# Channel sums in three halving additions and one place wait for two products, in a recommendation tower kernel

## The reference, cut to what matters

```python
# x0, xk: [batch, fields, 16]; w0: [39, 39, 128]; w1, w2: [39, 64, 128]
z = jnp.einsum('bhd,bkd,hks->bsd', x0, xk, W) + b[None, :, None]
z = jax.nn.relu(z)                      # [batch, 128, 16]
if idx != n_layers - 1:
    half = z.shape[1] // 2
    xk = z[:, :half, :]                 # input of the next layer
    direct.append(z[:, half:, :])       # goes to the output
else:
    direct.append(z)
logit = jnp.sum(jnp.concatenate(direct, axis=1), axis=-1)   # sum over the 16 channels d
```

## Time and profile before

| | |
|---|---|
| runs | 2479.24 us median, 2477.43 to 2480.89 |
| the profiled execution | 2478.53 us, of which the span is 2476.7 |
| busy in the span | PE 96%, DVE 94%, POOL 64%, ACT 44% |
| granted PE clock | 0.996 over the span |
| DMA | 193 GB/s over the span |
| a pass of the loop (two turns) | 144.96 us in the stretch shown below |

### The profile page before, as it was taken

The page is one execution under the profiler, slowest core; times in us unless marked ns, Lnnn a source line. Parts: engine busy times, 40 slices in busy tenths (PEclk is TensorE's granted clock), DMA queues, the critical chain, the costliest instruction groups (busy, mean ns, idle before and its releaser), DMA issues.

```text
span 2476.7 us, 29974 instructions
## 1 busy us (share of the span) xinstructions
PE 2377.4 (96%) x7700; PEld 1441.3 (58%) x7700; DVE 2325.5 (94%) x1596; ACT 1099.9 (44%) x1086; POOL 1591.8 (64%) x1027
## 2 busy tenths in 40 slices
PE   0799999999999999999999999999999999999989
PEld 0455555665555666555566555566656555665556
DVE  0799999999999999999999999999999999999992
ACT  0254443454444444444444444444444444444455
POOL 7877676766767676676777667677666757543340
PEclk9999999999999999999999999999999999999999
DMA  6888887988887898888889888888988888988720
GB/s 166 203 201 197 199 197 186 218 206 196 196 204 193 205 221 200 197 196 204 193 206 221 198 197 196 204 192 214 214 196 203 192 203 193 220 212 186 195 79 11
DMA packets 176749, 477.35 MB, mean 193 GB/s; under 512 B 31216, under 2 KB 65520, under 8 KB 176448
## 3 DMA queue, kind: packets, MB, share of 16 engines
q1 hardware_dynamic: 153073, 468.91, 77.7%
q0 software_dynamic: 19968, 5.15, 2.5%
q10 hardware_dynamic: 3680, 2.95, 0.5%
HBM read 464.57 MB, written 12.33 MB: 193 GB/s over the span
## 4 chain that ended last, share of the span: by engine, by line
PE 75%; DVE 8%; issue 4%; POOL 2%; ACT 2%; DMA 1%; SPq 0%; DVEq 0%; POOLq 0%; ACTq 0%
PE zacc_b L1035 31%; PE zacc_a L1035 28%; PE zacc_b L1074 6%; PE zacc_a L1074 6%; DVE prod L945 4%; DVE sums L957 2%; POOL low L672 1%; DVE high L904 1%; DMA shifted<-x_periods 1%; POOL landed L650 1%; ACT direct L777 1%; ACT maps L776 1%; PE zacc_b L1071 1%; PE zacc_a L1071 1%; DVE low L904 0%
## 5 line engine op out<-in xcount | busy, mean ns | idle before, releaser
L672 POOL TENSOR_TENSOR low<-prod,high 128x1024 fp32r<-128x1024 f32 x352 | 842.2, 2397 | 586.0 <-ACT high L835 582.4
L945 DVE TENSOR_TENSOR prod<-spread,maps 128x2048 f32<-128x2048 f32 x448 | 1018.6, 2280 | 17.6 <-issue 8.2
L835 ACT ACTIVATE high<-prod 128x1024 fp32r<-128x1024 f32 (+1 forms) x576 | 607.2, 1059 | 910.1 <-DVE prod L945 486.5
L650 POOL DMA_INDIRECT landed<-in_tbl,rows_id x585 | 685.7, 1172 | 175.1 <-issue 166.7
L1035 PE MATMUL zacc_a<-prod,w_plain 128*128 128x512 f32 (+1 forms) x1472 | 679.3, 596 | 20.5 <-DVE prod L930 11.1
L1035 PE MATMUL zacc_b<-prod,w_plain 128*128 128x512 f32 (+1 forms) x1472 | 677.6, 595 | 15.3 <-DVE prod L945 15.3
L1035 PEld LDWEIGHTS zacc_a<-prod,w_plain 128*128 128x128 f32 (+1 forms) x1472 | 278.1, 190 | 287.7 <-issue 251.9
L1035 PEld LDWEIGHTS zacc_b<-prod,w_plain 128*128 128x128 f32 (+1 forms) x1472 | 277.4, 190 | 282.5 <-issue 239.1
L1074 PE MATMUL zacc_b<-low,w_high 128*128 128x512 f32 x672 | 272.0, 490 | 4.3 <-POOL low L672 4.3
L1074 PE MATMUL zacc_a<-low,w_high 128*128 128x512 f32 x672 | 271.7, 489 | 0.0
L930 DVE TENSOR_TENSOR prod<-shifted,x_thrice 128x1024 f32<-128x1024 f32 (+1 forms) x192 | 225.1, 1215 | 15.0 <-DMA shifted<-x_periods 8.9
(11 more groups left out here) (106 smaller groups left out, 1856.3 us busy)
## 6 DMA issues: line engine op xcount, KB each, us to landing
spread<-x_periods SPq DMA_DIRECT2D x608, 512.0 KB, 9.9
shifted<-x_periods SPq DMA_DIRECT2D x188, 468.0 KB
x_thrice<-x_periods SPq DMA_DIRECT2D x93, 156.0 KB
landed<-in_tbl,rows_id POOLq DMA_INDIRECT x585, 5.2
spread<-x_periods SPq DMA_DIRECT2D x32, 256.0 KB, 21.2
x_periods<-x SPq DMA_DIRECT2D x30, 256.0 KB, 4.3
shifted<-x_periods SPq DMA_DIRECT2D x128, 44.0 KB
x_last<-x_periods SPq DMA_DIRECT2D x64, 80.0 KB
```

What stands on the lines that cost most here:

```text
L650: nc.gpsimd.indirect_dma_start(out=landed[:, f, :], out_offset=None, in_=tables[f], in_offset=bass.IndirectOffsetOnAxis(ap=rows[:, f:f + 1 ...
L672: nc.gpsimd.tensor_tensor(low[0:rows, at_, :], prod[0:rows, at_, :], high[0:rows, slot(j, SPLIT, NH), :], ALU.subtract).then_inc(s_lowp, 1)
L835: nc.scalar.activation(high[0:rows, h, :], made(turn, j)[0:rows, :], ACT.Copy).then_inc(s_round, 1)
L945: nc.vector.tensor_tensor(prod[:, at_:at_ + 2, :], spread[:, t:t + 2, :], maps[:, :].unsqueeze(1).to_broadcast([128, 2, COLS]), ALU.mult). ...
```

## The change

Three edits, all on DVE.

1. `channel_sum` becomes three steps of a halving sum in place. The first adds the upper 512 columns of `direct` to the lower 512, the second adds 256 columns to 256, the third adds 128 to 128 into `sums`. They run at three consecutive steps j (28, 29, 30 and 21, 22, 23), with a semaphore `s_half` between them. The wait for `s_feat` moves to the third.
2. In the turns of the loop (`not turn.fixed`) a product that goes to PSUM (D) no longer waits for its place; the product instruction in front of it waits for that place as well.
3. In those turns, squares 20, 22 and 24 wait for their own place and the next one's, and squares 21, 23 and 25 do not wait for a place.

```diff
+assert "D" not in (PLAN[OFFSET], PLAN[0], PLAN[LAST[0]])
...
+        s_half = sem("s_half")
...
                 to = made(turn, j)[0:rows, :]
-                held = [was for was in (before(turn, i, ALL, NP) for i in range(j, j + count)) if was]
+                upto = j + count
+                if not turn.fixed and PLAN[j] == "D":
+                    upto = j
+                elif not turn.fixed and upto < TILES and PLAN[upto] == "D":
+                    upto += 1
+                elif not turn.fixed and j in SQUARED:
+                    upto = j if (j - N1) % 2 else min(j + 2, SQUARED[-1] + 1)
+                held = [was for was in (before(turn, i, ALL, NP) for i in range(j, upto)) if was]
...
-            def channel_sum(turn, which):
+            def channel_sum(turn, which, step):
...
-                dve.wait_ge(ready, turn.count(1, 1))
-                if not turn.odd and (not turn.fixed or turn.number() > 0):
-                    dve.wait_ge(s_feat, turn.count(1, 0))
-                nc.vector.tensor_reduce(sums[:, which, turn.odd, :], src[:, :].rearrange("p (d b) -> p b d", b=ROWS), AX.X,
-                                        ALU.add).then_inc(done, 1)
+                if step == 0:
+                    dve.wait_ge(ready, turn.count(1, 1))
+                    nc.vector.tensor_tensor(src[:, 0:COLS // 2], src[:, 0:COLS // 2], src[:, COLS // 2:COLS], ALU.add
+                                            ).then_inc(s_half, 1)
+                elif step == 1:
+                    dve.wait_ge(s_half, turn.count(4, 2 * which + 1))
+                    nc.vector.tensor_tensor(src[:, 0:2 * ROWS], src[:, 0:2 * ROWS], src[:, 2 * ROWS:4 * ROWS],
+                                            ALU.add).then_inc(s_half, 1)
+                else:
+                    dve.wait_ge(s_half, turn.count(4, 2 * which + 2))
+
+                    if not turn.odd and (not turn.fixed or turn.number() > 0):
+                        dve.wait_ge(s_feat, turn.count(1, 0))
+                    nc.vector.tensor_tensor(sums[:, which, turn.odd, :], src[:, 0:ROWS], src[:, ROWS:2 * ROWS],
+                                            ALU.add).then_inc(done, 1)
...
-                if turn.real() and j == SUM01_AT:
-                    channel_sum(turn, 0)
+                if turn.real() and 0 <= j - SUM01_AT < 3:
+                    channel_sum(turn, 0, j - SUM01_AT)
...
-                if last.real() and j == sum2_at:
-                    channel_sum(last, 1)
+                if last.real() and 0 <= j - sum2_at < 3:
+                    channel_sum(last, 1, j - sum2_at)
```

## The result

The changed kernel takes 2493.67 us, the median of four runs (2489.89 to 2494.45), against 2478.34 for the kernel before on the same chip (four runs, 2476.40 to 2480.89). The ratio is 1.0058, with a 95% interval of 1.0041 to 1.0076: 0.6% slower. I had forecast 2474.9 with a range of 2460 to 2486, so the time lies outside it, on the side of rival C. The profiled execution took 2489.89, its span is 2488.1.

A forecast was written before the change was run, and what follows sets the result against it. PE was taken as the bound, with a small loss at one hand-over per turn. Fourteen odd loop turns at 0.09 (1.3 us), even turns 0 and turns outside the loop 3.0 made 4.3 us, so 2474.9 us, range 2460 to 2486.

The forecast's parts named there:

- rival C: Slower: in the loop DVE or PE gets its answer later by x, paid in 27 turns; 2488 at x = 0.5; chance 0.15.
- What bounds the kernel: Whole loop: PE is the bound, losing 0.95 us at tile 29 in odd turns and 0.23 in even ones.
- rival B: Tile 13: the new wait does not bind or its delay is absorbed, 19.3 us gained, 2459.9; chance 0.2.
- The additions: Channel sums on DVE: 0.69, 0.42 and 0.285 us replace each reduction, and DVE gains 1.24 us per turn.
- The gate at the pair 13 and 14: Every loop turn: this DVE pair now waits for PE's step 9, answered 0.27 us after the next matmul's start.
- P13's loss of 0.24: PE at P13, both kinds of turn: the late pair 13 and 14 makes ACT's result late, 0.24 us lost.
- The delay of 2.04: Pair 13 and 14, every loop turn: DVE starts it at 1202.08 instead of 1200.04, 2.04 us later.
- All DVE work up to tile 29: DVE behind the gate, odd turn: additions fill the DMA wait; tile 27 is 0.86 us late, replacing 0.95 at tile 29.
- The even turn: Even loop turns, tile 27: 0.21 us late, covered by P13's 0.24, against 0.23 lost today; nothing gained.
- Waits removed give nothing: D products and squares: DVE runs products 1.13 us apart whether they wait or not, so dropping waits gains nothing.
- rival D: Additions: three instructions with semaphores issue slowly; at 0.2 us per turn 2.8 of the 4.3 are gone, 2478; chance 0.15.
- Turns outside the loop: Old waits stay there: turn 1 gains 0.8 us, turn 30 0.85, turn 2 1.0, turn 0 about 0.3; together 3.0.

The follow-up runs named there:

- waits alone: The kernel before with its reductions kept and all waits for ring places changed as in the changed kernel: 2536.79 us, ratio 1.0230.
- experiment 4: The kernel before with its reductions and all changed waits but tile 15's: 2496.68 us, ratio 1.0022.

## Why the prediction was wrong, point by point

- **What bounds the kernel** (PE, with a loss at tile 29 of the odd turn): right. With the losses gone a pass is 143.9 us, and the kernel takes 2460, where rival B's sum gave 2459.9.
- **The additions** (0.69, 0.42, 0.285; a gain of 1.24 per turn): right, 0.692, 0.417 and 0.287, and 20 us when they act alone. The instruction behind a short addition starts 0.08 before its end (1153.06 + 0.28 to 1153.26), as I had read it in the rows before. The prediction called that a contradiction to the Trainium skill ("VectorE: DVE Perf Modes", section "The DRAIN you can't avoid"), and left out what the same section adds: a next operation that is not held starts earlier. The trace agrees with that addition.
- **The gate at the pair 13 and 14**: right in place, cause and latency (0.26 against 0.27). P13's loss of 0.24 is 0.22. The delay of 2.04 costs 2.05 per turn where no work is saved behind it (waits alone).
- **The step that failed** is in "All DVE work up to tile 29": "square 26 could start at 1223.84. Its load is issued when square 22 is made (...) so 1223.98: the additions fill the DMA wait." I took one load out of the three that are issued during the squares. Square 25's, of 468 KB and issued behind square 24's, was at no place in the sum, though two of 21 turns of the kernel before show a wait for it. Undisturbed, square 25 starts 7.0 us after square 20 is made (1221.08 to 1228.05) where it was 7.65 (1213.72 to 1221.37), and the load isn't any sooner. By the trace's landing events its last part lands, on the mean of the 21 turns, 7.57 us after square 20 is made in the kernel before (6.97 to 8.25) and 7.74 in the changed one (7.03 to 8.51); in the turn shown it let the square start at 8.35 (1147.42 to 1155.77). So the load is as late as it was, and its reader comes 0.65 earlier; the trace of the kernel before had this number. The mis-sized term is this DMA wait at square 25: taken as 0, measured 8.94 - 8.28 = 0.66 per turn. (All waits of the squares for loads are 19.8 us in 28 places; they were 13.6 in 31, most of them at square 26, where the sum had the load.) As the pair 27 and 28 had no slack after the gate, PE pays: 146.27 - 144.91 = 1.36 us per pass, 14 passes 19.0 us. The forecast of 2474.9 and these 19.0 make 2493.9; measured 2493.67. That it fits to 0.2 us is luck: without the term the kernel takes 2471.85, 3 us under the forecast, and 22 us, not 19, lie between these two kernels.
- **The even turn** ("P13's 0.24 covers it ... Nothing is gained") fell by the same term: it has waits at tile 27 as well.
- **Waits removed give nothing**: about right as time (experiment 4 has them cost 0.2%), and incomplete. They are 12 instructions less in DVE's loop body, and without them the first edit alone is 125 us slower instead of 20 faster. No term, bound or rival of mine had this; rival D came near in words (three instructions issue slowly) and was not it.
- **Rival C**, the slower side, was priced by latency x, which kept its 0.27. The side was right, the mechanism wrong: its chance of 0.15 should have been on any transfer that now has less time.
- **Turns outside the loop**: the waits of turns 1 and 30 are gone, as forecast. In turn 2 the one at tile 29 is gone, but PE now waits as long (0.75 us, at 276.91) at tile 27, behind a wait of 0.90 for square 25's load: of the 1.0 forecast for this turn little is left.

## What to carry to other kernels

When work moves closer together, list every transfer that is issued and used in between, with its landing, not the one that waits today: a load that was just in time is the next wait. A wait may be merged forward only where what stands in front of it has slack; here moving five of the six D tiles' waits and the squares' cost 0.2% at most, and the sixth D tile's 33 to 37 us. In a loop, count the engine's instructions before adding any, and if a kernel gets slower by some 11 us per pass with an idle time that nothing is seen to have ended, look at the instruction queues: the same work can be 6% slower by its place in the stream. The version to keep is the additions with tile 15's own wait, 2460.44 us, 0.75% faster than before.

## What the runs showed of the hardware

- A loop body of 266 instructions on DVE cost 145 us more or not by 16 instructions ahead of it (2604.81 and 2459.61); each pass then fetched five more packets and held DVE for 7.35 and 4.38 us behind the jump back.
- An idle time of PE of 6.53 us was followed by a granted clock of 0.58 over the next 6 us. The waits of 0.2 to 1.4 us in the changed kernel left it at 1.00.
- Cutting square 25's load from 468 KB to 12 KB took 1.36 us off a pass (146.27 to 144.91); cutting it and square 24's in the kernel before took nothing (145.14 both): here the transfer cost only where it was the last to come.
- The last part of that load lands 7.0 to 8.5 us after the event that lets the first of two such loads be issued, in both kernels.
